# Node work moved into the attention loop, one-hots by scalar comparisons, and softplus's positive part kept in PSUM, in a four-layer graph network kernel

## The reference, cut to what matters

```python
# layer 0: attention over the incoming edges, 8 heads of 16
q, k, v = x @ Wq + bq, x @ Wk + bk, x @ Wv + bv
alpha = softmax over a node's edges of (q[dst] . (k[src] + w * We)) / 4
h = sum over edges of alpha * (v[src] + w * We)
h = h + x @ Wskip + bskip                 # heads joined
y = h @ Wo + bo
x = layernorm(x + gamma * norm(x + y) + beta)
# layer 1: edge MLP (32 edge features), segment sum, update, norm
hidden = relu(x[src] @ W1s + x[dst] @ W1d + e32 @ W1e + b1)
# layer 2: filter network (50 edge features)
W = (softplus(e50 @ mlp_w0 + mlp_b0) - log 2) @ mlp_w2 + mlp_b2
msg = 0.5 * (cos(pi * w / 10) + 1) * W * h1[src]; agg = segment_sum(msg, dst)
# layer 3: gated graph layer, means over both directions, GRU cell
```

## Time and profile before

| | us |
|---|---|
| median of three runs | 6397.5 (6388.44 to 6406.57) |
| the profiled execution's own time | 6392.59 |
| its span, first to last instruction | 6390.8 |
| attention gathers issued, 121 to 1288 | 1167 |
| end of attention loop to first gather of the edge loop | 237 |
| edge loop's gathers, 1572 to 2772 | 1200 |
| filter loop's gathers, 2818 to 3972 | 1154 |

### The profile page before, as it was taken

One profiled execution on the slowest core, in us unless ns is written; L12 is line 12 of the kernel. 1 busy time (PEld: TensorE's weight loads), 2 busy tenths in 40 slices (PEclk: granted clock), 3 DMA queues, 4 the chain that ended last, 5 costly groups with the idle time before them and its releaser, 6 DMA issues. The chain is left out here.

```text
span 6390.8 us, 90868 instructions
## 1 busy us (share of the span) xinstructions
PE 3964.4 (62%) x20362; PEld 3198.7 (50%) x20362; DVE 3646.1 (57%) x10637; ACT 2759.1 (43%) x6616; POOL 4510.8 (71%) x4587
## 2 busy tenths in 40 slices
PE   5666666633666666668888888343444446666565
PEld 4555666532555555546655555333333346664443
DVE  6777777777878888756666666111101034445555
ACT  3788888822111111245555554111111158873333
POOL 2777777723777777757777776677777777777664
PEclk8787777866888888877788887555555579987777
DMA  4444444522655555542222224322222245552113
GB/s 123 123 130 130 132 132 128 127 35 57 197 135 136 135 137 138 141 74 69 71 71 71 71 71 57 96 77 77 76 76 76 73 120 166 167 162 64 51 50 40
DMA packets 479907, 649.20 MB, mean 102 GB/s; under 512 B 119419, under 2 KB 325898, under 8 KB 479382
## 3 DMA queue, kind: packets, MB, share of 16 engines
q0 software_dynamic: 155552, 345.75, 21.6%
q1 hardware_dynamic: 323831, 297.64, 17.0%
HBM read 495.50 MB, written 150.71 MB: 101 GB/s over the span
## 5 line engine op out<-in xcount | busy, mean ns | idle before, releaser
L677 POOL DMA_INDIRECT e_ring<-table,gather_i x880 | 932.2, 1059 | 286.4 <-issue 266.8
L677 POOL DMA_INDIRECT e_ring<-filter_rows,gather_i x880 | 886.3, 1007 | 305.0 <-issue 267.7
L1980 POOL DMA_INDIRECT rows_by_src<-rs_out,key x880 | 866.0, 984 | 320.6 <-issue 259.3
L677 POOL DMA_INDIRECT gl_ring_f<-table,gather_i x880 | 855.6, 972 | 333.4 <-issue 249.9
L677 POOL DMA_INDIRECT kv_ring<-keys_values,gather_i x880 | 875.9, 995 | 297.9 <-issue 238.0
L1950 PE MATMUL rs_ph<-nodes,rs_hot_t 128*128 x1760 | 449.2, 436 | 681.5 <-ACT rs_out L1967 657.5
L1950 PEld LDWEIGHTS rs_ph<-nodes,rs_hot_t 128*128 128x128 f32 x1760 | 387.1, 324 | 744.0 <-issue 744.0
L1911 DVE TENSOR_SCALAR rs_hot_t<-rs_rows,part 128x512 f32<-128x512 bf16 x220 | 113.0, 515 | 983.5 <-PE rs_ph L1950 967.5
L1364 PE MATMUL e_pa<-e_msg,e_hot 128*128 128x128 f32 x3520 | 573.0, 315 | 145.5 <-DVE e_msg L1557 141.1
L1364 PEld LDWEIGHTS e_pa<-e_msg,e_hot 128*128 128x128 f32 x3520 | 521.4, 227 | 174.7 <-DVE e_msg L1557 170.1
L2119 PE MATMUL gl_sum_f<-gl_ring_f,gl_hot_f 128*128 128x128 f32 x1760 | 297.9, 323 | 466.2 <-DVE arena L2166 274.1
(11 more groups left out here) (449 smaller groups left out, 9657.4 us busy)
## 6 DMA issues: line engine op xcount, KB each, us to landing
rows_by_src<-e_filler SPq DMA_DIRECT2D x256, 260.0 KB
arena<-rows_by_src SPq DMA_DIRECT2D x256, 260.0 KB
at_rows<-local_rows SPq DMA_DIRECT2D x220, 128.0 KB
e_rows<-local_rows SPq DMA_DIRECT2D x220, 128.0 KB
rs_rows<-local_rows SPq DMA_DIRECT2D x220, 128.0 KB
e_attr<-edge_attr SPq DMA_DIRECT2D x880, 25.0 KB
kv_ring<-keys_values,gather_i POOLq DMA_INDIRECT x880
e_ring<-table,gather_i POOLq DMA_INDIRECT x880
```

The source lines that it names most:

```text
L677: pool.indirect_dma_start(ring[:, r, u, :], None, table, bass.IndirectOffsetOnAxis(index, 0)).then_inc(arrived[r], 16)
L1980: pool.indirect_dma_start(table, bass.IndirectOffsetOnAxis(place, 0), out[:, r, u, :], None, bounds_check=SLOTS_R - 1, oob_is_err=False).t ...
```

## The change

**Attention.** The blocks between the attention loop and the edge layer's set-up are gone: "heads", "wo", the norm, "l1in". Their work is now done for one bucket at a time in the attention loop, beginning one slot after the bucket's last add, at eight fixed lags: DVE joins the heads (lag 1), PE turns them and adds the skip rows (2), multiplies with Wo and adds bias and x (3), DVE and ACT do the first norm (4, 5), the second (5, 6), PE turns the new rows (7) and projects them with W1 (8). ACT takes each product out of PSUM. SP fetches a bucket's skip rows and stores its projected rows. The slots run to 237, from 229. The chain's two PSUM tiles are now one (`p_turn = p_row`), which frees the bank for the node products. The weights of the later layers are loaded in one block. **Counts.** The sources are loaded in the setup and counted beside the first projection; the destinations, being sorted, are counted from which of 128 chunks of 832 are wholly below a bound, and one product and one counting pass per half for the chunk that is cut. **Edge loop.** Its one-hot of 128x512 is made by four comparisons of 128x128 with a scalar per partition. **Filter loop.** ACT writes the positive part over `pt` in PSUM, after its own |x| has been taken, DVE reads it there, and PE's next product into that buffer waits for DVE's `soften`.

```diff
-def count_bucket(c, dve, key, counts, junk, counted, b):
+def count_sources(c, dve, junk, counted, k):
+    if k < NB:
+        at_least(dve, counted, k, None)
+        dve.tensor_scalar(junk, c.src_f, c.bounds[:, bass.ds(k, 1)], 0.0, ALU.is_lt, ALU.add, accum_out=c.src_counts[:, bass.ds(k, 1)]).then_inc(counted, 1)
...
# stage_lists: dve, then pe
+            for h in range(2):
+                done(dve.tensor_scalar(junk[0:NB, h, :], psw[0:NB, h, 0:CHUNK // 2], s[:, 7:8], 0.0, ALU.is_lt, ALU.add, accum_out=s[:, 5 + h:6 + h]))
...
+            for h in range(2):
+                ins = pe.matmul(psw[0:NB, h, 0:CHUNK // 2], c.open[:, :], c.dst_f[:, h * CHUNK // 2:(h + 1) * CHUNK // 2], start=True, stop=True)
...
+NODE_AT = [BUCKET_ENDS[n] + LAG + 1 for n in range(NB)]
+JOIN, TURNED, MIXED, FIRST, SECOND, RENEWED, AGAIN, PROJECTED = 1, 2, 3, 4, 5, 6, 7, 8
...
# stage_attention, pe: called behind query(s), ahead of the chain's parts and total(s - LAG)
+            def turn_heads(n):
+                pe.wait_ge(joined, n + 1)
+                pe.wait_ge(skipped[n % 2], 16 * (n // 2 + 1))
+                pe.matmul(pn[:, 0, :], h[:, :], c.ident[:, :], start=True, stop=False)
+                return pe.matmul(pn[:, 0, :], skip[:, n % 2, :], c.ident[:, :], start=False, stop=True)
+            def mix_heads(n):
+                of = of_nodes(n)
+                pe.matmul(pn[:, 1, :], c.ones_bf[:, :], bias(c, "L0_bo"), start=True, stop=False)
+                pe.matmul(pn[:, 1, :], h_t[:, :], c.w["wo"][:, :], start=False, stop=False)
+                return pe.matmul(pn[:, 1, :], c.ident[:, :], of, start=False, stop=True)
+            def turn_nodes(n):
+                pe.wait_ge(renewed, n + 1)
+                return pe.matmul(pn[:, 2, :], x_new[:, :], c.ident[:, :], start=True, stop=True)
...
# act: called last in the slot
+            def inverse_root(n, w):
+                act.wait_ge(moments, 2 * n + w + 1)
+                act.activation(root[:, w, 0:1], mean[:, w, 1:2], ACT.Ln, bias=c.eps[:, 0:1]).then_inc(rooted, 1)
+                act.wait_ge(rooted, 4 * n + 2 * w + 1)
+                act.activation(root[:, w, 1:2], root[:, w, 0:1], ACT.Exp, scale=-0.5).then_inc(rooted, 1)
+            def take_nodes(s):
+                due = [node_due(s, lag) for lag in (TURNED, MIXED, AGAIN, PROJECTED)]
+                if any(n is not None for n in due):
+                    act.wait_ge(given, node_groups_before(s + 1))
+                if due[0] is not None:
+                    act.activation(h_t[:, :], pn[:, 0, :], ACT.Copy).then_inc(taken, 1)
...
# dve: called last in the slot
+            def join_heads(n):
+                at = bucket_in_turn(nc, c, n, DVE_ENGINE)
+                dve.wait_ge(added, U * (BUCKET_ENDS[n] + 1))
+                dve.tensor_scalar(den[:, 0, :], of_bucket(acc, at, C_EX, C_EW), 1e-16, None, ALU.max).then_inc(denominated, 1)
+                dve.tensor_tensor(by_head, spread(of_bucket(acc, at, C_EW, C_CNT)), c.w["we"][:, :].rearrange("p (h d) -> p h d", d=D), ALU.mult).then_inc(denominated, 1)
...
+            def second_norm(n):
+                dve.wait_ge(rooted, 4 * n + 2)
...
# stage_edges, filter layer
-                act.activation(pos[:, q, :, :], x, ACT.Relu, bias=c.w["mlp_b0"][:, 0:1]).then_inc(copied, 1)
-                at_least(act, copied, 4 * k + 1, tick)
+                act.wait_ge(copied, 4 * k + 1)
+                act.activation(x, x, ACT.Relu, bias=c.w["mlp_b0"][:, 0:1]).then_inc(copied, 1)
...
# pe, turn: the product pt of batch k
-                at_least(pe, copied, 4 * (k - 1), tick)
+                at_least(pe, second, k - 1, tick)
...
# edge layer
-                    dve.tensor_tensor(hot[:, r, :, :], over(c.j[:, 0:P], U), wide(local[:, bass.ds(k * U, U)], P), ALU.is_equal).then_inc(hots, 1)
-                return [edges_hot]
+                    dve.tensor_scalar(hot[:, r, u, :], c.j[:, 0:P], local[:, bass.ds(k * U + u, 1)], None, ALU.is_equal).then_inc(hots, 1)
+                return [lambda u=u: edge_hot(u) for u in range(U)]
...
# soften
-in0=pos[:, q, :, :].rearrange("p u f -> p (u f)"),
+in0=pt[:, q, :, :].rearrange("p u f -> p (u f)"),
...
# attention_layer: gone
-        vector_scalar_stage(nc, c, "heads", [
-        sweep(nc, c, "wo", [(lambda k: at_tile(heads, k), P)], [(None, bias(c, "L0_bo"), 0, F), (0, c.w["wo"][:, :], 0, F)],
-        norm_stage(nc, c, "norm0", y, heads, small, affine=(c.w["gamma"][:, :], c.w["beta"][:, :]), plus=arena(c, ACC0, [NT, F]))
# edge_mlp_layer: gone
-        sweep(nc, c, "l1in", [(lambda k: at_tile(c.x, k), P)],
```

More of the change, by code:

```diff
@@ L274, in stage_lists @@
         M = {name: n + 1 for n, name in enumerate([
-            "ends", "starts", "row", "first", "cols", "order", "bucket", "turnedsrc", "turneddst", "turnedw"])}
+            "chunks", "starts", "row", "first", "cols", "order", "bucket", "turnedsrc", "turneddst", "turnedw"])}
         @block.vector
@@ L803, in _ @@
                     sp.dma_start(pen[:, n % 2, 0:P], breaks).then_inc(pens_in[n % 2], 16)
+            sp.wait_ge(padded, 16)
+            for q in range(2):
+                sp.wait_ge(row_sent[q], 16 * len(range(q, NB, 2)))
         @block.tensor
@@ L1076, in _, with renew_nodes @@
+            def renew_nodes(n):
+                dve.wait_ge(rooted, 4 * n + 4)
+                at_least(dve, replaced, n, None)
+                dve.tensor_scalar(x_new[:, :], z[:, :], mean[:, 1, 0:1], root[:, 1, 1:2], ALU.subtract, ALU.mult).then_inc(renewed, 1)
             for s in range(SLOTS_N):
@@ L1109, in _ @@
                     add(ka, 3, which[3])
+                for lag, part in ((RENEWED, renew_nodes), (SECOND, second_norm), (FIRST, first_norm), (JOIN, join_heads)):
+                    if node_due(s, lag) is not None:
+                        part(node_due(s, lag))
             dve.wait_ge(added, BATCHES * U)
+            dve.tensor_copy(c.count[:, :], acc[:, :, C_CNT]).then_inc(counted, 1)
 def stage_edges(nc, c, name, table, acc, buckets, local, layer, h1, next_rows=None):
@@ L1714, in attention_layer @@
                       lambda e, k, po, ring: e.activation(at_tile(q_full, k, 0, F), po[:, 0:F], ACT.Copy, scale=1.0 / D ** 0.5)],
-              store=keep, beside=lambda dve, k: count_bucket(c, dve, c.dst_f, c.dst_counts, junk, counted, k))
+              store=keep, beside=lambda dve, k: count_sources(c, dve, junk, counted, k))
         stage_lists(nc, c, t, q_full)
-        stage_attention(nc, c)
-        src_i, src_f = arena(c, QUERY0, [CHUNK], I32), arena(c, B1_0 + NT * F, [CHUNK])
-        load_whole(nc, c, arena(c, B2_0, [NT, F]), c.skip, "skip", also=(src_i, c.src.rearrange("(p n) -> p n", p=P)))
@@ L1744, in load_whole @@
-def load_whole(nc, c, to, table, name, also):
-    with ExitStack() as ctx:
-        loaded = c.semaphore(name + "_loaded")
-        block = ctx.enter_context(nc.Block())
-        @block.sync
-        def _(sp):
-            sp.dma_start(to, table.rearrange("t p f -> p t f")).then_inc(loaded, 16)
-            sp.dma_start(*also).then_inc(loaded, 16)
-            sp.wait_ge(loaded, 32)
+        small_weights = []
+        for n, held in (("w1s", "wq"), ("w1d", "wk")):
+            c.w[n] = c.w[held]
+            small_weights.append((c.w[n][:, :], t["L1_" + n]))
@@ L1849, in _ @@
             def _(sp):
+                for to, of in loads:
+                    sp.dma_start(to, of).then_inc(placed, 16)
                 sp.wait_ge(cleared, 1)
```

199 lines of the change are left out of this document (143 added, 56 removed).

## The result

The changed kernel takes 6231.9 us (median of three runs, 6229.97 to 6235.4) against 6397.5: a ratio of 0.9745, 95% interval 0.9732 to 0.9758, so 166 us less where 223 were forecast. Its profiled execution took 6235.4 us, 157 less than the one of before.

| stretch | before | after | difference | forecast |
|---|---|---|---|---|
| start to first attention gather (setup, projection, lists) | 120.7 | 126.4 | +5.7 | +8.7 |
| first attention gather to the loop's last add | 1213.8 | 1289.3 | +75.5 | +25 |
| last add to first edge gather (glue) | 237.1 | 40.0 | -197.1 | -202 |
| edge loop's gathers | 1200.2 | 1194.2 | -6.0 | -20 |
| filter loop's gathers | 1154.3 | 1108.3 | -46.0 | -35 |

A forecast was written before the change was run, and what follows sets the result against it. Bounds: POOL's gathers and issue in the edge loops, and 237 us of glue without edge work. 6392.6 - 202 + 3.4 + 5.3 + 25 - 20 - 35 = 6169.3, 6174 as median; own range 6145 to 6210, whole 6118 to 6262.

The forecast's parts named there:

- rival C: Edge and filter loops: gathers do not shorten, as PE bounds or narrow comparisons collide too; 6229 or 6259 us; chance 0.17.
- an attention loop that grows by more than 75 us: Attention loop: growth beyond this would show the forecast wrong, as would a glue gap that is not most of the gain.
- Glue: Between attention and edge loops: 35 us left of 237, for last bucket's chain, block end, weights and lists; -202, bounds -185 to -209.
- Setup and lists: Before the first attention gather: loading the sources +3.4 us, new search for destinations +5.3, bounds 2 and 9.
- Attention loop: Per-bucket node work, 176 us of DVE, barely fits 163 us of waiting for gathers; +25 us, bounds 0 and +176.
- rival B: Attention loop becomes bound by its chain across engines, 2.5 us per bucket, 122 us instead of 25; 6271 us; chance 0.18.
- 27 us of waits for PE and 9 of collisions: Attention loop: products ahead of PE's turns hold DVE 0.5 us in 53 instances; POOL collides with more two-SBUF-input DVE operations.
- The wait that the text expected to grow: Attention loop: sign that DVE's wait for PE's turns grows from 1.1 to about 1.6 us each.
- Edge loop: Four narrow one-hot comparisons replace the wide one, so POOL's gathers shorten; -20 us, bounds -40 and +30.
- The mean gather was to fall to about 1035 ns: Edge loop: sign of shorter gathers, from 1059 ns; if the mean stays, it is rival C.
- Filter loop: `soften` has one input in PSUM instead of two in SBUF, so gathers shorten; -35 us, bounds -50 and +10.
- The +10 for PE's wait: Filter loop: upper bound, PE's wait for `soften` showing in 1 of 4 batches.

The follow-up runs named there:

- e5: The changed kernel without DVE's register loads in the attention loop, buckets and places written as numbers: ratio 0.9632, 6158.4 us; attention gathers span 1166.7 us.
- e11: The changed kernel with DVE's attention-loop register loads behind two different long instructions, the 128x512 reduction and the 128x512 message: ratio 0.9661, 6184.6 us.
- e13: The changed kernel with e11's loads, PE's node products behind the chain's turns and e12's ones in PSUM together: ratio 0.9573, 6127.6 us.
- e2: The changed kernel with ACT's two inverse roots per bucket moved from a slot's end to the middle of the next: ratio 0.9739, 6243.6 us.
- e6: The changed kernel with six of DVE's 13 node instructions per bucket left out: ratio 0.9653, 6167.4 us; attention gathers span 1169.2 us.
- e8: The changed kernel with the edge loop's ranking scan, product and sum done over 8 columns instead of 832: ratio 0.9617, edge gathers 1115.0 us.
- e9: As e8, with the edge loop's one-hot made by one 128x512 comparison again: ratio 0.9639, edge gathers span 1135.4 us.
- e10: The changed kernel with softplus's positive part in SBUF again, as before the change: ratio 0.9805, 6276.0 us; filter loop 1151.3 us.
- e12: The changed kernel with the constant ones of the edge loop's 49 scans read from PSUM: ratio 0.9648, 6177.9 us; edge loop 1141.5 us.
- e1: The changed kernel with DVE's attention-loop register loads moved ahead of the last add, behind the 128x512 message: ratio 0.9693, 6216.2 us.

## Why the prediction was right, and where its sum was off

The time fell into the whole range, 6118 to 6262, and lies 58 us above the forecast, outside the forecast's own range of 6145 to 6210. The gain comes where the text said, from the glue and the filter loop; the attention loop and the edge loop came out worse. That 6232 is next to rival C's 6229 is chance: C's gathers that stay long can be at most the 14 us of the edge loop. One of the text's own signs of being wrong was met by a hair, an attention loop that grows by more than 75 us: 75.5 to its last add, 66.6 between its first and last gather. Taken step by step:

- **Glue**, -202: measured -197. The last bucket's chain and the block's end make 20 us of the 40 (1415.7 to 1436.0), where 16.5 had been worked out, weights and lists 19.7 (19 forecast).
- **Setup and lists**, +8.7: measured +5.7, inside the bounds.
- **Attention loop**, +25: measured +75, between the forecast and rival B. This is the term that was mis-sized, by 50 us, and most of the miss. It was also chosen and not added up: 27 us of waits for PE and 9 of collisions already make 36. Its parts can be read off. DVE's node instructions last 3.5 us per bucket in all, 3.3 from start to start, close to the 3.6 worked out: busy time rose by 143 us. The 163 us of waiting for gathers did cover it: 153 of them were used up. The waits for PE grew by 16, less than the 27 allowed. The wait that the text expected to grow, at L1180, fell from 1.1 to 0.8 us each, but L1161 and L1149 wait now. What the sum lacked was the register loads, a term put at nothing without a word. Every slot has one, and it was hidden inside the message; the change put short node instructions ahead of it, and further loads between them. DVE's "issue" went from 21 us to 73, and what of it stands behind loads from nothing to 65. The prediction counted DVE's 13 instructions per bucket, those with a row in the trace. e5 bounds the price of loads and register operations together at 67 us; e11 shows that placing the loads alone recovers 47, and e13 another 9.5 by PE's turns. The last 10 of the 66.6 are not assigned.
- **Rival B**, the chain across engines with ACT's roots: the size of the loop's growth went halfway to it (75 of 122), and one of its marks came true, POOL waiting 99 us for ACT. Yet the mechanism is not it: moving the roots gives 0 us (e2), and e6 and e11, which leave the steps across engines in place and shorten DVE's slot, give 64 and 47 and shrink that wait to 30 and 39. The releaser that POOL's row names was one step away from the cause.
- **Edge loop**, -20: measured -6. The size of the one-hot's share was about right (20.4 by e8 and e9, 22 to 24 by sorting the gathers), at or below the 25 to 35 of the text; that it equals the -20 to the microsecond is luck. What the step left out is the ranking, by far the larger part of the excess, whose long operations collide at other moments once the batch is laid out otherwise, 85 us instead of 65. Why their phase is worse is not settled; eight profiles agree that it is. The mean gather was to fall to about 1035 ns and fell to 1052.
- **Filter loop**, -35: measured -46, near the floor; e10 gives 43 for its undoing. About 10 of the 46, and 3 of the 43, are the shorter unlengthened gather, so `soften` is worth some 36 to 40, by the mechanism named. The +10 for PE's wait did not come: PE is busy 914 of 1109 us, 82%, and not the 88% worked out, at a granted clock of 0.84 against 0.81.
- **Rival C**: `soften`'s gathers did shorten, so for the filter loop it falls. The row of e12 is direct: two SBUF inputs hold a gather off, one input in PSUM does not. But the reading on which both terms rest, that scalar comparisons don't collide, was half wrong. They do: a gather that begins well inside one of 0.48 or 0.65 us ends 0.81 to 0.82 us after it, as with two SBUF inputs. The pair of the earlier trace rows could hardly show it, as its comparisons last 0.34 us. By the same numbers, as an estimate, one of 0.28 us can add at most 0.1 us to a gather of 0.94 (0.28 + 0.82, less the first 0.07 us, in which a beginning gather escapes). So the four narrow one-hots cost 3 us in 880 gathers because they are short, and the form of the one-hot may not be what gained; no run here has a wide one-hot by a scalar comparison.

  The Trainium skill, page "SBUF — State Buffer", section "Who interferes with whom", has 2-port modes, which `tensor_scalar` can enter, block GpSimd. The trace agrees as far as it goes: the 128x832 comparison takes 0.65 us, where the product of the same shape takes 1.01, and holds the gather. The same section has two SBUF inputs contend with GpSimd's reads, with which e12 agrees. From its inference that descriptor generation is spared the prediction took that `soften` would gain nothing, and that did not hold; whether it is the descriptors or the reading of the indices that waits, no trace here shows.

For the load itself the same notes had a price: the Trainium skill, page "DMA: Bandwidth & Descriptors", section "Latency and other measured facts", gives a `tensor_load` a floor of about 0.6 us. The gap of 0.61 us before L1224 agrees, but the trace records the loads themselves with 0.34 to 0.60 us, 0.34 for most of those before the change. An estimate by the page's figure, 0.6 us for each of two extra loads per bucket, would have added 59 us to the forecast, 6233. That this is the measured time is in part luck, since it counts only the extra loads, while the ones that every slot had cost as much once short instructions stood ahead of them.

## What to carry to other kernels

Count an in-order engine's register loads when work is moved to it: they have no row, they show only as "issue" idle, and in this loop each was hidden when an instruction of about 0.7 us of its own stood ahead of it. Where a loop is set by indirect gathers, look at what DVE runs as a gather starts. Give the longest operations with two SBUF inputs one in PSUM, even if that is only a constant. A long scalar comparison holds gathers too, so having only one SBUF input is not enough by itself. And when a releaser names an engine, ask whether that engine was itself late, and move its work in one run to see.

## What was not expected of the hardware

- A gather that starts inside a DVE operation with two SBUF inputs lasts until that operation ends and 0.75 to 0.83 us more: the scan of the changed kernel's pair above ends at 2008.71, the gather at 2009.46. In each of the 49 scans of that loop one gather was held, and it ended 0.75 to 0.76 us after its scan. Six more began within the first 0.06 us of a scan and took 0.94 all the same. For `soften` before the change it was 0.82 to 0.83 us (49 of 49 gathers begun well inside it). A scalar comparison with one SBUF input does the same, at 0.81 to 0.82 us (28 of 28 in e8); an operation with one input in PSUM doesn't. So the price goes with the operation's length, and the 49 scans of 1.94 us cost more than the 220 one-hots of 0.68.
- One register load hides whole behind a 128x512 instruction of 0.68 us (207 of 210 before the change); with two in a row 0.43 us is left over (e1, 94 times).
- A scan reads one broadcast column of PSUM as fast as one of SBUF, 1.94 us for 128x832.
